# Selective scan of a four-layer network: products made by TensorE, transposing sums, decay factors in SBUF

## The chip, the cores and the metric

The program runs on one core of one Trainium2 chip, in fp32. The metric is the device time of one execution in microseconds (us).

## The reference, cut to what matters

The program computes eight sub-layers in a row (four pairs of a token mixer and a feed-forward part, each with a residual and a layer norm) on a state of 2 x 1024 tokens by 1024 features. The change lies in the mixer of the third pair, a selective scan over time for 2048 channels with 16 states each:

```python
def step(h, inp):
    x_t, dt_t, B_t, C_t = inp
    dA = jnp.exp(dt_t[..., None] * A)
    dBx = dt_t[..., None] * B_t[:, None, :] * x_t[..., None]
    h = dA * h + dBx
    y = jnp.einsum('bdn,bn->bd', h, C_t)
    return (h, y)
h0 = jnp.zeros((x.shape[0], x.shape[1], A.shape[1]), dtype=x.dtype)
_, ys = lax.scan(step, h0, (xT, dtT, BT, CT))
```

The scan's result then gets `D * x` added and is gated by silu(z).

## The kernel before, in words

`l2_scan` (L2552) holds 128 channels on the partitions and 512 tokens on the free axis. The tokens come in CHUNKS = 4 chunks of 512 (chunks 0 and 2 begin a sequence, chunks 1 and 3 start from the saved end state `carry`), the channels in CT = 16 tiles. One tile of one chunk is an **item**; there are 64. The 16 states of an item are taken in pairs (SGR = 2): eight **steps** g = 0 to 7 in an item, 512 steps in all.

One step passes five engines:

- ScalarE makes the decay factors of the pair, two exponentials 128x512 (L2820), into the PSUM ring of five banks.
- GpSimd multiplies dt*x (`dtx`, L2841) by two rows of B, one operation 128x1024 from SBUF into a slot of `h` in SBUF (`make_dBx`, L2851). It runs LEAD = 3 steps ahead; `h` has SLOTS = 6 slots.
- VectorE runs the recurrence, two instructions tensor_tensor_scan (L2921): decay factors from the PSUM ring, products from `h`.
- The product with C follows `KINDS = "YWYWYWYY"`. In a **Y** step VectorE scans into the PSUM ring and multiplies by C into `h` (L2932). In a **W** step it scans into `h`, and GpSimd multiplies `h` by C in place (L2876).
- TensorE adds the pair up in PSUM (`total`, L2753): the identity as weights, 128x512 of `h` moving, two matmuls.

Beside the steps, each item has: TensorE's matmul for dt (L2733) and eight for the gate z (L2743), from chunk 1 on eight matmuls of the output projection of the chunk before (L2538, `OutProj`, whose operands come through a ring of three buffers); ScalarE's softplus and silu (`split`, `log1p`, `gate` with its two table loads L2806 and L2807); VectorE's `pre_c` and `pre_dt` (L2888, L2893), `finish` (L2899, L2902) and, every second item, an addition to the state (L2549); GpSimd's `low` (L2834) and `dtx_`.

Each engine follows an order written by hand, one loop over the steps. GpSimd's loop in step st: `low` (g = 4), `dtx_` (g = 5), `make_dBx(st + 3)`, then in a W step the product with C, which waits for VectorE's scans of that step. In the text below M is such a product with C, and m a product with B. `gate(q - 1)` stands on ScalarE between the exponentials of g = 1 and g = 2 of item q.

In this kernel every instruction of VectorE in the scan that has two tensor inputs takes one of them from PSUM and one from SBUF.

## Time and profile before

| what | value |
|---|---|
| median of 3 runs | 5360.51 us (5357.15 to 5362.31) |
| the profiled execution | 5354.56 us, of which the span is 5352.8 us |
| busy over the whole span | TensorE 92%, VectorE 61%, ScalarE 35%, GpSimd 43% |
| granted TensorE clock, mean | 0.961 |
| the scan | from about 2384 us to 4254 us, more than a third of the span |
| products with B (GpSimd, L2851) | 512, mean 2358 ns |
| products with C (GpSimd, L2876) | 192, mean 2355 ns |
| scans (VectorE, L2921) | 1024, 1205 to 1273 ns |

The shares over the whole span say little: the four engines are busy in different stages. What a change in the scan is worth is read in the scan's own stretch, where the time of one item on each engine can be taken from the starts of its instructions. A start-to-start distance is used for the cost of an instruction where the engine runs without a gap, since the printed durations overlap a little.

### The profile page before, as it was taken

To read this page: it belongs to the slowest core of one execution; us is meant where nothing else is said; L and a number is where in the kernel's file an instruction comes from. 1 tells how busy PE (TensorE), PEld (TensorE's weight loads), DVE (VectorE), ACT (ScalarE), POOL (GpSimd) and SP (SyncE) were. 2 spreads that over 40 slices of the span, in tenths; PEclk is the share of its full clock that TensorE was granted. 3 is DMA by queue.
4 is the path that set the end of the run, shared out by engine and by line. 5 is a ranking of instruction groups with operands and counts; after the bars stand their busy time and mean duration, and the time that the engine had idled before them with its cause. 6 is when DMAs were issued, how large, how long until landed. Compare 5 with 4: busy or idle time off the path is not lost. (4 is left out here: it accounts for less than half of the span.)

```text
span 5352.8 us, 40461 instructions
## 1 busy us (share of the span) xinstructions
...
## 2 busy tenths in 40 slices
...
DMA packets 180006, 360.84 MB, mean 67 GB/s; under 512 B 21790, under 2 KB 56734, under 8 KB 175710
## 3 DMA queue, kind: packets, MB, share of 16 engines
...
## 5 line engine op out<-in xcount | busy, mean ns | idle before, releaser
L2851 POOL TENSOR_TENSOR l2scan_h<-l2scan_dtx,l2scan_Bb 128x1024 f32<-128x1024 f32 x512 | 1198.2, 2358 | 30.8 <-DMA l2scan_Bb<-l_bc 15.0
L2753 PE MATMUL l2scan_yp<-l2scan_h,ident 128*128 128x512 f32 x2048 | 971.5, 608 | 115.1 <-POOL l2scan_h L2876 101.1
L2820 ACT ACTIVATE l2scan_ring<-l2scan_dt,l2scan_A 128x512 f32<-128x512 f32 x1024 | 663.9, 681 | 639.4 <-DVE l2scan_h L2932 481.0
L2753 PEld LDWEIGHTS l2scan_yp<-l2scan_h,ident 128*128 128x128 f32 x2048 | 389.3, 193 | 639.4 <-issue 481.1
L2743 PE MATMUL l2scan_low_z<-state,l2scan_Wz 128*128 128x512 f32 x1024 | 476.6, 598 | 0.3
L2876 POOL TENSOR_TENSOR l2scan_h<-l2scan_h,l2scan_Cb 128x1024 f32<-128x1024 f32 x192 | 452.1, 2355 | 8.6 <-DVE l2scan_h L2921 0.9
L2411 PE MATMUL l2in_acc<-state,l2in_W 128*128 128x512 f32 x1024 | 444.9, 595 | 10.5 <-DMA l2in_W<-l_attn_in_x 10.5
L2932 DVE TENSOR_TENSOR l2scan_h<-l2scan_ring,l2scan_Cb 128x1024 f32<-128x1024 f32 (+1 forms) x384 | 394.3, 1041 | 6.1 <-DMA l2scan_Cb<-l_bc 0.7
L2921 DVE TENSOR_TENSOR_SCAN l2scan_ring<-l2scan_ring,l2scan_carry,l2scan_h 128x512 f32<-128x512 f32 x320 | 392.7, 1273 | 0.0
L2921 DVE TENSOR_TENSOR_SCAN l2scan_ring<-l2scan_ring,l2scan_h 128x512 f32<-128x512 f32 x320 | 373.3, 1212 | 5.5 <-POOL l2scan_h L2851 5.5
L2538 PE MATMUL l2scan_oacc<-l2scan_oy,l2scan_oW 128*128 128x512 f32 x768 | 353.1, 592 | 0.0
L2743 PEld LDWEIGHTS l2scan_low_z<-state,l2scan_Wz 128*128 128x128 f32 x1024 | 197.1, 193 | 256.6 <-issue 255.8
L2411 PEld LDWEIGHTS l2in_acc<-state,l2in_W 128*128 128x128 f32 x1024 | 194.4, 190 | 258.7 <-issue 247.4
L2467 DVE TENSOR_SCALAR l2in_cv<-l2in_xp,l2in_cw,l2in_cb 128x2048 f32<-128x2048 f32 (+1 forms) x17 | 21.8, 1284 | 397.5 <-ACT l2in_xc L2431 354.3
L2921 DVE TENSOR_TENSOR_SCAN l2scan_h<-l2scan_ring,l2scan_carry,l2scan_h 128x512 f32<-128x512 f32 x192 | 235.2, 1267 | 0.0
L2538 PEld LDWEIGHTS l2scan_oacc<-l2scan_oy,l2scan_oW 128*128 128x128 f32 x768 | 145.9, 190 | 183.7 <-issue 183.4
L2198 PE MATMUL l3pair_bank<-state,l3ffn_W 128*128 128x512 f32 x512 | 225.6, 593 | 0.0
L2921 DVE TENSOR_TENSOR_SCAN l2scan_h<-l2scan_ring,l2scan_h 128x512 f32<-128x512 f32 x192 | 223.5, 1205 | 0.6 <-POOL l2scan_h L2851 0.6
L3061 PE MATMUL l2pair_bank<-state,l2ffn_W 128*128 128x512 f32 x512 | 221.6, 592 | 0.0
L2443 ACT ACTIVATE l2in_xp<-l2in_acc 128x512 f32<-128x512 f32 x64 | 38.2, 598 | 482.6 <-PE l2in_acc L2411 482.6
L713 DVE TENSOR_REDUCE l0att_part<-l0att_SB 128x1 f32<-128x512 f32 x192 | 130.9, 690 | 71.9 <-PE l0att_SB L879 71.4
L148 POOL TENSOR_TENSOR l1proj_part<-state 128x1024 f32<-128x1024 f32 x3 | 7.0, 2349 | 383.1 <-DVE state L1704 383.1
...
## 6 DMA issues: line engine op xcount, KB each, us to landing
l2scan_oy<-l_y SPq DMA_DIRECT2D x192, 512.0 KB, 4.9
...
l2scan_oW<-l_attn_out_w SPq DMA_DIRECT2D x192, 128.0 KB, 3.3
...
l2scan_Bb<-l_bc SPq DMA_DIRECT2D x128, 128.0 KB, 6.9
l2scan_Cb<-l_bc SPq DMA_DIRECT2D x128, 128.0 KB, 7.8
...
```

The lines of the kernel that those rows point to most:

```text
L713: v.tensor_reduce(part[:, H % 2, i // 2, i % 2:i % 2 + 1], SB[:, i % 2, :], AX.X, ALU.max, negate=True).then_inc(max_ok, 1)
L2198: t.matmul(acc, self.W[:, k, m * P:(m + 1) * P], x[:, k, :], start=k == 0, stop=False)
L2411: last = t.matmul(acc[:, n % 4, :], W[:, ct % 2, k, :], x[:, k, :], start=k == 0, stop=k == KT - 1)
L2538: last = t.matmul(self.acc, self.W[:, j, k], self.y[:, j, k], start=kp == 0 and k == 0, stop=kp == PIECES - 1 and k == PIECE - 1)
L2743: last = t.matmul(low_z[:, :], Wz[:, q % 2, k, :], x[:, k, :], start=k == 0, stop=k == KT - 1)
L2753: last = t.matmul(yp[:, :], K.ident[:, :], h[:, st % SLOTS, j, :], start=g == 0 and j == 0, stop=g == NSG - 1 and j == SGR - 1)
L2820: a.activation(bank(st, j), dt[:, q % 2, :], ACT.Exp, scale=A[:, ct, n:n + 1]).then_inc(dA_ok, 1)
L2851: g_.tensor_tensor(h[:, st % SLOTS], dtx[:, None, :].to_broadcast([P, SGR, NT]), Bb[:, g * SGR:(g + 1) * SGR, :], ALU.mult).then_inc(dBx_o ...
L2876: g_.tensor_tensor(hs, hs, Cb[:, g * SGR:(g + 1) * SGR, :], ALU.mult).then_inc(hC_g, 1)
L2921: last = v.tensor_tensor_scan(out, bank(st, j), hs[:, j, :], init, ALU.mult, ALU.add)
L2932: last = v.tensor_tensor(hs[:, js], src, Cb[:, g * SGR + js.start:g * SGR + js.stop, :], ALU.mult)
L3061: last = t.matmul(acc, self.W[:, k, m * P:(m + 1) * P], x[:, k, :], start=k == 0, stop=k == KT - 1)
```

## The change

Three things change in `l2_scan`, and buffers move to make room.

1. **Who makes dt*x*B.** Of the eight pairs, two (g = 2 and g = 6, `MAKERS = "PPTPPPTP"`) are made by TensorE. `turn_dtx` transposes dt*x once an item (4 transposes 128x128), ScalarE copies it to SBUF (`keep_dtx`), and `spread` multiplies it with diagonal matrices of B (8 matmuls 128x128 with 128 columns), so that the product comes out with the channels on the partitions, in the PSUM ring. ScalarE makes the diagonals once a chunk (`columns`, `diagonals`: 16 copies 128x128). In these steps the decay factors go to the slot of `h` in SBUF.
2. **The sums.** `total` takes `h` as weights and the identity as moving operand, with is_transpose: 8 passes of 128 columns in place of 2 matmuls of 512 columns. The sum stands transposed in PSUM (`yT`); ScalarE copies it (`keep`), and TensorE turns it back (`turn_back`, 4 transposes). `finish` moves from after g = 1 to after g = 2.
3. **Kinds and buffers.** `KINDS` becomes "YWYWYWYW": one pair more is multiplied by C on GpSimd. The PSUM ring becomes two pairs for the Y steps only. The decay factors of the W steps go to an SBUF buffer of two pairs, `dAw`. `ssm` has one buffer and the ring of the output projection two.

```diff
-KINDS = "YWYWYWYY"
+KINDS = "YWYWYWYW"
+MAKERS = "PPTPPPTP"
...
-        self.RING = 3
+        self.RING = 2
...
-    BANKS = 5
+    PAIRS = 2
...
-        Bb = s.sb("Bb", [P, NS, NT])
+        Bb = s.sb("Bb", [P, SGR * MAKERS.count("P"), NT])
...
+        ysb = l[:, :].rearrange("p (k d) -> p k d", d=P)
+        BT = s.sb("BT", [P, BLOCKS, NS])
+        dtxT = s.sb("dtxT", [P, BLOCKS, P])
+        dg = s.sb("dg", [P, SGR * MAKERS.count("T"), BLOCKS, P])
+        dAw = s.sb("dAw", [P, PAIRS, SGR, NT])
+        ring = s.ps("ring", [P, PAIRS, SGR, NT])
+        yT = s.ps("yT", [P, BLOCKS, P])
...
+        def made(k, st):
+            q, g = divmod(st + 1, NSG)
+            return q * MAKERS.count(k) + MAKERS[:g].count(k)
...
+        def pair(st):
+            return (upto(kind(st), st) - 1) % PAIRS
...
+            return ring[:, pair(st), j, :]
+
+        def wait_pair(e, st):
+            k = kind(st)
+            n = upto(k, st) - PAIRS
+            if n <= 0:
+                return
+            if k == "Y":
+                e.wait_ge(hC_v, n)
+            else:
+                e.wait_ge(h_ok, max(i for i in range(st) if kind(i) == "W" and upto("W", i) == n) + 1)
...
+                        t.wait_ge(copied, q)
+                    for j in range(SGR):
+                        for k in range(BLOCKS):
+                            last = t.matmul(yT[:, k, :], h[:, st % SLOTS, j, k * P:(k + 1) * P], K.ident[:, :], is_transpose=True,
+                                            start=g == 0 and j == 0 and k == 0, stop=g == NSG - 1 and j == SGR - 1 and k == BLOCKS - 1)
+                    last.then_inc(summed, 1)
...
+                def turn_dtx(q):
+                    t.wait_ge(dtx_ok, q + 1)
+                    if q % CT == 0:
+                        t.wait_ge(bt_ok, q // CT + 1)
+                    if q >= 2:
+                        t.wait_ge(y_ok, q - 1)
+                    elif q:
+                        t.wait_ge(dx_ok, q)
+                    for k in range(BLOCKS):
+                        last = t.transpose(yp[:, k * P:(k + 1) * P], dtx[:, k * P:(k + 1) * P], K.ident[:, :])
+                    last.then_inc(dx_ready, 1)
+
+                def spread(st):
+                    q, g = divmod(st, NSG)
+                    n = made("T", st)
+                    t.wait_ge(dg_ok, q // CT + 1)
+                    t.wait_ge(dx_ok, q + 1)
+                    wait_pair(t, st)
+                    for j in range(SGR):
+                        i = SGR * MAKERS[:g].count("T") + j
+                        for k in range(BLOCKS):
+                            last = t.matmul(bank(st, j)[:, k * P:(k + 1) * P], dtxT[:, k, :], dg[:, i, k, :], start=True, stop=True)
+                    last.then_inc(dBxT_ok, 1)
+
+                def turn_back(q):
+                    t.wait_ge(copied, q + 1)
+                    t.wait_ge(dx_ok, min(q + 2, ITEMS))
+                    if q:
                         t.wait_ge(y_ok, q)
-                    for j in range(SGR):
-                        last = t.matmul(yp[:, :], K.ident[:, :], h[:, st % SLOTS, j, :], start=g == 0 and j == 0, stop=g == NSG - 1 and j == SGR - 1)
-                    last.then_inc(summed, 1)
+                    for k in range(BLOCKS):
+                        last = t.transpose(yp[:, k * P:(k + 1) * P], ysb[:, k, :], K.ident[:, :])
+                    last.then_inc(turned_back, 1)
...
+                    if g == 2 and q:
+                        turn_back(q - 1)
...
+                    if st + 1 < STEPS and maker(st + 1) == "T":
+                        spread(st + 1)
...
+                    if g == 6 and q + 1 < ITEMS:
+                        turn_dtx(q + 1)
...
+                def keep(q):
+                    a.wait_ge(summed, (q + 1) * NSG)
+                    a.wait_ge(dt_ok, min(q + 2, ITEMS))
+                    if q:
+                        a.wait_ge(turned_back, q)
+                    a.activation(ysb[:, :, :], yT[:, :, :], ACT.Copy).then_inc(copied, 1)
...
+                def keep_dtx(q):
+                    a.wait_ge(dx_ready, q + 1)
+                    if q:
+                        a.wait_ge(dBxT_ok, made("T", q * NSG - 1))
+                    a.activation(dtxT[:, :, :], yp[:, :].rearrange("p (k d) -> p k d", d=P), ACT.Copy).then_inc(dx_ok, 1)
...
+                def diagonals(c):
+                    a.wait_ge(bt_ok, c + 1)
+                    if c:
+                        a.wait_ge(dBxT_ok, made("T", c * CT * NSG - 1))
+                    for g in range(NSG):
+                        if maker(g) == "P":
+                            continue
+                        for j in range(SGR):
+                            i, n = SGR * MAKERS[:g].count("T") + j, g * SGR + j
+                            for k in range(BLOCKS):
+                                last = a.activation(dg[:, i, k, :], K.ident[:, :], ACT.Copy, scale=BT[:, k, n:n + 1])
+                    last.then_inc(dg_ok, 1)
...
+                    if maker(st) == "P":
+                        wait_pair(a, st)
+                        decay = ring[:, pair(st)] if kind(st) == "Y" else dAw[:, pair(st)]
+                    else:
+                        if st >= SLOTS:
+                            a.wait_ge(summed, st - SLOTS + 1)
+                        decay = h[:, st % SLOTS]
                     for j in range(SGR):
                         n = g * SGR + j
-                        wait_bank(a, st, j)
-                        a.activation(bank(st, j), dt[:, q % 2, :], ACT.Exp, scale=A[:, ct, n:n + 1]).then_inc(dA_ok, 1)
+                        a.activation(decay[:, j, :], dt[:, q % 2, :], ACT.Exp, scale=A[:, ct, n:n + 1]).then_inc(dA_ok, 1)
                     if g == 1 and q:
+                        keep(q - 1)
...
+                    if g == 7 and q + 1 < ITEMS:
+                        keep_dtx(q + 1)
+                        if (q + 1) % CT == 0:
+                            diagonals((q + 1) // CT)
...
+                    if maker(st) == "T":
+                        return
...
-                    v.wait_ge(summed, (q + 1) * NSG)
+                    v.wait_ge(turned_back, q + 1)
...
-                        last = v.tensor_tensor_scan(out, bank(st, j), hs[:, j, :], init, ALU.mult, ALU.add)
+                        if maker(st) == "T":
+                            dA, dBx = hs[:, j, :], bank(st, j)
+                        else:
+                            dA, dBx = bank(st, j) if kind(st) == "Y" else dAw[:, pair(st), j, :], hs[:, j, :]
...
-                        for js, src in runs(st):
-                            last = v.tensor_tensor(hs[:, js], src, Cb[:, g * SGR + js.start:g * SGR + js.stop, :], ALU.mult)
-                        last.then_inc(hC_v, 1)
-                    if g == 1 and q:
+                        v.tensor_tensor(hs, ring[:, pair(st)], Cb[:, g * SGR:(g + 1) * SGR, :], ALU.mult).then_inc(hC_v, 1)
+                    if g == 2 and q:
                         finish(q - 1)
```

The order of GpSimd over one item of chunk 1, from its dt*x (L2841) on. The rows name line, operation, output and inputs. Before:

```order
L2841 TENSOR_TENSOR l2scan_dtx<-l2scan_dt,l2scan_xc 128x512
L2851 TENSOR_TENSOR l2scan_h<-l2scan_dtx,l2scan_Bb 128x1024
L2876 TENSOR_TENSOR l2scan_h<-l2scan_h,l2scan_Cb 128x1024
L2851 TENSOR_TENSOR l2scan_h<-l2scan_dtx,l2scan_Bb 128x1024 x4
L2876 TENSOR_TENSOR l2scan_h<-l2scan_h,l2scan_Cb 128x1024
L2851 TENSOR_TENSOR l2scan_h<-l2scan_dtx,l2scan_Bb 128x1024 x2
L2876 TENSOR_TENSOR l2scan_h<-l2scan_h,l2scan_Cb 128x1024
L2834 TENSOR_TENSOR l2scan_l<-l2scan_l,l2scan_dt 128x512
L2851 TENSOR_TENSOR l2scan_h<-l2scan_dtx,l2scan_Bb 128x1024
```

The same stretch now (L2970 is dt*x, L2982 a product with B, L3007 one with C):

```order
L2970 TENSOR_TENSOR l2scan_dtx<-l2scan_dt,l2scan_xc 128x512
L2982 TENSOR_TENSOR l2scan_h<-l2scan_dtx,l2scan_Bb 128x1024
L3007 TENSOR_TENSOR l2scan_h<-l2scan_h,l2scan_Cb 128x1024
L2982 TENSOR_TENSOR l2scan_h<-l2scan_dtx,l2scan_Bb 128x1024
L3007 TENSOR_TENSOR l2scan_h<-l2scan_h,l2scan_Cb 128x1024
L2982 TENSOR_TENSOR l2scan_h<-l2scan_dtx,l2scan_Bb 128x1024 x2
L3007 TENSOR_TENSOR l2scan_h<-l2scan_h,l2scan_Cb 128x1024
L2982 TENSOR_TENSOR l2scan_h<-l2scan_dtx,l2scan_Bb 128x1024
L3007 TENSOR_TENSOR l2scan_h<-l2scan_h,l2scan_Cb 128x1024
L2962 TENSOR_TENSOR l2scan_l<-l2scan_l,l2scan_dt 128x512
L2982 TENSOR_TENSOR l2scan_h<-l2scan_dtx,l2scan_Bb 128x1024
```

Eight products with B became six and three with C became four, and behind at most two products with B there is now one with C, which waits for VectorE.

VectorE's order from the end of `finish` on (the scans are printed there as SCALAR_TENSOR_TENSOR; L3059 is the scan, L3067 the product with C), now:

```order
L3033 TENSOR_TENSOR l2scan_zs<-l2scan_zs,l2scan_yp 128x512
L3059 SCALAR_TENSOR_TENSOR l2scan_h<-l2scan_dAw,l2scan_carry,l2scan_h 128x512 x2
L3019 SCALAR_TENSOR_TENSOR l2scan_low_z<-l2scan_low_z,l2scan_u 128x512
L3059 SCALAR_TENSOR_TENSOR l2scan_ring<-l2scan_ring,l2scan_carry,l2scan_h 128x512 x2
L3067 TENSOR_TENSOR l2scan_h<-l2scan_ring,l2scan_Cb 128x1024
L3024 TENSOR_TENSOR l2scan_dt<-l2scan_l,l2scan_low_z 128x512
L3059 SCALAR_TENSOR_TENSOR l2scan_h<-l2scan_dAw,l2scan_carry,l2scan_h 128x512 x2
L3059 SCALAR_TENSOR_TENSOR l2scan_ring<-l2scan_h,l2scan_carry,l2scan_ring 128x512 x2
L3067 TENSOR_TENSOR l2scan_h<-l2scan_ring,l2scan_Cb 128x1024
```

Before, the scan of a W step was `l2scan_h<-l2scan_ring,l2scan_carry,l2scan_h`, one input in PSUM; now both inputs, `dAw` and `h`, lie in SBUF. In a step of TensorE's pairs the two inputs changed places, and one of them is still in PSUM.

ScalarE's order from the exponentials of g = 0 to those of g = 3, now:

```order
L2940 ACTIVATE l2scan_ring<-l2scan_dt,l2scan_A 128x512 x2
L2940 ACTIVATE l2scan_dAw<-l2scan_dt,l2scan_A 128x512 x2
L2886 ACTIVATE l2scan_l<-l2scan_yT 128x512
L2892 ACT_TABLE_LOAD
L2892 ACTIVATE l2scan_zs<-l2scan_low_z 128x512
L2893 ACT_TABLE_LOAD
L2940 ACTIVATE l2scan_h<-l2scan_dt,l2scan_A 128x512 x2
L2940 ACTIVATE l2scan_dAw<-l2scan_dt,l2scan_A 128x512 x2
```

The copy of the transposed sum (L2886) is new and stands ahead of the gate and of the exponentials of g = 2; it waits for the last sum of the item before.

## Rows read from the trace of the kernel before

**Rows 1.** Windows: busy us of each engine in a stretch of chunk 0 and chunk 1

```profile
core 0: us, PE busy (x) PEld busy (x) DVE busy (x) ACT busy (x) POOL busy (x), PEclk, DMA share, GB/s
2600.00:2700.00 100.00, 79.39 (x173) 31.83 (x171) 94.60 (x111) 59.80 (x88) 98.38 (x57) 0.98 0.18 45
3000.00:3100.00 100.00, 100.00 (x235) 44.22 (x233) 98.80 (x95) 57.49 (x83) 99.13 (x47) 1.00 0.40 121
```

**Rows 2.** Timeline of VectorE in one item of chunk 1: start, length, instruction

```profile
3012.24 2.46 DVE L2921 TENSOR_TENSOR_SCAN l2scan_ring<-l2scan_ring,l2scan_carry,l2scan_h 128x512 f32<-128x512 f32 x2
...
3015.88 2.45 DVE L2921 TENSOR_TENSOR_SCAN l2scan_h<-l2scan_ring,l2scan_carry,l2scan_h 128x512 f32<-128x512 f32 x2
...
3022.86 0.68 DVE L2893 TENSOR_TENSOR l2scan_dt<-l2scan_l,l2scan_low_z 128x512 f32<-128x512 f32 x1
3023.45 2.45 DVE L2921 TENSOR_TENSOR_SCAN l2scan_h<-l2scan_ring,l2scan_carry,l2scan_h 128x512 f32<-128x512 f32 x2
3025.82 2.44 DVE L2921 TENSOR_TENSOR_SCAN l2scan_ring<-l2scan_ring,l2scan_carry,l2scan_h 128x512 f32<-128x512 f32 x2
...
3029.44 0.68 DVE L2549 TENSOR_TENSOR state<-l2scan_oacc,state 128x512 f32<-128x512 f32 x1
3030.04 2.46 DVE L2921 TENSOR_TENSOR_SCAN l2scan_ring<-l2scan_ring,l2scan_carry,l2scan_h 128x512 f32<-128x512 f32 x2
...
3039.67 0.73 DVE L2899 SCALAR_TENSOR_TENSOR l2scan_yp<-l2scan_xc,l2scan_Dp,l2scan_yp 128x512 f32<-128x512 f32 x1
...
3041.04 2.46 DVE L2921 TENSOR_TENSOR_SCAN l2scan_ring<-l2scan_ring,l2scan_carry,l2scan_h 128x512 f32<-128x512 f32 x2
```

**Rows 3.** Timeline of GpSimd in the same item

```profile
3011.85 2.35 POOL L2876 TENSOR_TENSOR l2scan_h<-l2scan_h,l2scan_Cb 128x1024 f32<-128x1024 f32 x1
3014.16 4.75 POOL L2851 TENSOR_TENSOR l2scan_h<-l2scan_dtx,l2scan_Bb 128x1024 f32<-128x1024 f32 x2
...
3021.18 1.27 POOL L2834 TENSOR_TENSOR l2scan_l<-l2scan_l,l2scan_dt 128x512 f32<-128x512 f32 x1
3022.41 2.36 POOL L2851 TENSOR_TENSOR l2scan_h<-l2scan_dtx,l2scan_Bb 128x1024 f32<-128x1024 f32 x1
3024.93 1.27 POOL L2841 TENSOR_TENSOR l2scan_dtx<-l2scan_dt,l2scan_xc 128x512 f32<-128x512 f32 x1 [0.17 <-POOL l2scan_h L2851]
3026.28 2.35 POOL L2851 TENSOR_TENSOR l2scan_h<-l2scan_dtx,l2scan_Bb 128x1024 f32<-128x1024 f32 x1
```

**Rows 4.** Lines L2899 and L2921: count, min/median/max ns, first and last start

```profile
L2899 DVE SCALAR_TENSOR_TENSOR l2scan_yp<-l2scan_xc,l2scan_Dp,l2scan_yp x64: 727/731/757, 2429.7 to 4252.5; 128x512 f32<-128x512 f32 x64
...
L2921 DVE TENSOR_TENSOR_SCAN l2scan_h<-l2scan_ring,l2scan_carry,l2scan_h x192: 1255/1266/1278, 2862.0 to 4237.6; 128x512 f32<-128x512 f32 x192
```

**Rows 5.** VectorE, line L2019 of another stage: its summary and two of its instructions

```profile
L2019 DVE SCALAR_TENSOR_TENSOR state<-l1ffn_os,l1ffn_b,state x32: 751/753/2626, 1592.9 to 1778.4; 128x512 f32<-128x512 f32 x32
...
1641.01 1.46 DVE L2019 SCALAR_TENSOR_TENSOR state<-l1ffn_os,l1ffn_b,state 128x512 f32<-128x512 f32 x1
...
1684.51 2.60 DVE L2019 SCALAR_TENSOR_TENSOR state<-l1ffn_os,l1ffn_b,state 128x512 f32<-128x512 f32 x1
```

**Rows 6.** Timeline of GpSimd at the same places

```profile
1639.52 2.40 POOL L163 TENSOR_TENSOR l1ffn_sq<-l1ffn_sq 128x1024 f32<-128x1024 f32 x1 [7.31 <-ACT l1ffn_sq L219]
1641.87 2.86 POOL L165 TENSOR_TENSOR l1ffn_sq<-l1ffn_sq 128x1024 f32<-128x1024 f32 x1
...
1684.22 2.34 POOL L154 TENSOR_TENSOR l1ffn_part<-l1ffn_part 128x1024 f32<-128x1024 f32 x1
```

**Rows 7.** Timeline of TensorE in the attention of the last pair

```profile
4822.68 1.04 PE L3176 MATMUL l3att_tp<-ident,l3att_E 128*128 128x128 f32 x8
4823.55 3.74 PE L3186 MATMUL l3att_op<-l3att_PT,l3qkv_vt 128*128 128x128 f32 x32
```

**Rows 8.** Groups of ScalarE by line and shape in the scan, 2600 to 4180 us

```profile
L2820 ACT ACTIVATE l2scan_ring<-l2scan_dt,l2scan_A 128x512 f32<-128x512 f32 x873 | 565.7, 681 | 513.5 <-DVE l2scan_h L2932 392.5 <-DVE l2scan_h L2921 119.2
L2807 ACT ACT_TABLE_LOAD x55 | 70.6, 1283 | 1.0
...
L2806 ACT ACTIVATE l2scan_zs<-l2scan_low_z 128x512 f32<-128x512 f32 x55 | 32.8, 597 | 22.5 <-PE l2scan_low_z L2743 21.4
```

**Rows 9.** Windows of two other stages, for the granted clock

```profile
100.00:150.00 50.00, 40.57 (x131) 23.09 (x130) 20.39 (x28) 10.22 (x19) 2.68 (x10) 0.61 0.00 0
4815.00:4940.00 125.00, 121.31 (x756) 92.35 (x754) 44.18 (x92) 32.91 (x47) 0.10 (x1) 1.00 0.00 1
```

More of the change, by code:

```diff
@@ L2583, in l2_scan @@
         xc_in = [s.sem(f"xc_in{j}") for j in range(3)]
-        ssm_in = [s.sem(f"ssm_in{j}") for j in range(2)]
+        ssm_in = s.sem("ssm_in")
         c_in = [s.sem(f"c_in{g}") for g in range(NSG)]
@@ L2732, in dt_tile @@
                         t.wait_ge(dt_ok, q)
-                    t.matmul(low_z[:, :], Wdt[:, q % 2, :], ssm[:, c % 2, :], start=True, stop=True).then_inc(dt_ready, 1)
+                    t.matmul(low_z[:, :], Wdt[:, q % 2, :], ssm[:, :], start=True, stop=True).then_inc(dt_ready, 1)
                 def z_part(q, k0, k1):
```

82 lines of the change are left out of this document (54 added, 28 removed).

## The prediction

> **What bounds the kernel now.** I looked first at the windows of the scan. In chunk 1 the busy times of 100 us are TensorE 100, GpSimd 99.1 and VectorE 98.8, ScalarE 57 [rows 1]: three engines are full together. In chunk 0, without the output projection, TensorE is busy 79% and GpSimd 98%. Next the length of an item: the first of the 64 `finish` starts at 2429.7 us, the last at 4252.5 [rows 4], so an item takes 1822.8 / 63 = 28.93 us. Then the timelines of one item, read from start to start.
>
> VectorE: a Y step costs 3015.88 - 3012.24 = 3.64 us, a W step 3025.82 - 3023.45 = 2.37, `finish` 1.37, `pre_dt` 0.59 (I take 0.6 for `pre_c` and the addition, of the same size) [rows 2]. Five Y, three W, 1.37, 1.2 and half an addition are 28.2 us.
>
> GpSimd: an operation 128x1024 costs 3014.16 - 3011.85 = 2.31 us, `low` 1.23, dt*x 1.35 and 0.17 ahead of it [rows 3]. Eleven and these are 28.2 us.
>
> TensorE: 235 records in 100 us are 0.4255 us each [rows 1], two to an fp32 matmul, so 0.851 for 512 columns. An item has 1 + 8 + 8 + 16 = 33: 28.1 us, and 21.3 in chunk 0.
>
> **The change, engine by engine.** TensorE: eight transposes start at 4822.68 and what follows them at 4823.55, so one costs 0.109 us, and the 32 records of 16 small matmuls take 3.74 [rows 7]. Eight sums of eight passes are 64 x 0.109 = 7.0 us in place of 16 x 0.851 = 13.6. Two `spread` of 16 records add 3.7, the transposes of dt*x and back 0.9. With 17 large matmuls (14.5) an item is 26.1 us, 19.3 in chunk 0.
>
> GpSimd: six products with B and four with C are 10 x 2.31 = 23.1, with 2.75 for the rest 25.9 us.
>
> VectorE: one Y step becomes a W step: 4 x 3.64 + 4 x 2.37 + 1.37 + 1.2 + 0.3 = 26.9 us, if nothing makes it wait.
>
> By these sums alone an item would fall from 28.9 to about 27 us. ScalarE gets two copies of 0.68 more (its 128x512 exponential to PSUM, mean 681 ns [rows 8]) on 57% of busy time.
>
> **Where a new wait comes from.** The W steps' scans now have both inputs in SBUF, and there are eight an item. The scan stage before has no such instruction, so I looked for one beside a working GpSimd. Line L2019 adds two tensors in SBUF. Its median is 753 ns and its longest 2626 [rows 5]. The long ones lie exactly on GpSimd's operations: one issued at 1684.51, 0.29 us after GpSimd had begun an operation that ended at 1684.22 + 2.34 = 1686.56; it ended at 1687.11, 0.55 us after that [rows 5, 6]. The other way round: one issued at 1641.01 ended at 1642.47, when GpSimd had finished at 1641.92, and GpSimd's next operation, issued at 1641.87, took 2.86 us in place of 2.35 and ended 2.26 us after VectorE's [rows 5, 6]. So the two shut each other out for a whole instruction, and VectorE, waiting, goes ahead of GpSimd's next. An instruction that has waited then takes 0.2 us less than its printed time (0.55 for 0.75), so a scan with carry takes 1.266 - 0.2 = 1.07 us after its wait [rows 4], a GpSimd operation 128x1024 about 2.26.
>
> The Trainium skill (SBUF — State Buffer, Who interferes with whom) states the same as a rule against this change: a VectorE instruction with two SBUF inputs contends with a GpSimd instruction that reads SBUF, and the second to issue is blocked fully. By that rule the item is the one worked out next; without it, that of the first rival. For L2019 the trace agrees (2.60 against 0.75 us); for a scan no run here shows it yet.
>
> **An item with that exclusion**, from the orders of the two engines, each part counted from the end of the W step before. M is a product with C, m one with B; an M starts 0.1 us (my estimate) after the scans it waits for.
> - To the end of W1: VectorE wants it after Y0, at 3.64. GpSimd has M7 to 2.41 and m3 to 4.72. Scan one ends at 5.79, m4 at 8.05, scan two at 9.12.
> - W3: wanted after Y2 and `finish`, at 5.01. GpSimd has M1 and m5, ends at 4.72 and then waits for M3. No collision: 7.38.
> - W5: wanted at 0.6 + 3.64 + 0.59 = 4.83. GpSimd: M3 2.41, `low` 3.64, m7 5.95. Scan one 7.02, dt*x 8.2, scan two 9.27.
> - W7: wanted at 3.94. GpSimd: the blocked m0 2.26, M5 4.57. Scan one 5.64, m1 7.9, scan two 8.97.
>
> The sum is 34.7 us. What stands behind a waiting scan on VectorE (the next Y step, `finish`, `pre_dt`) is late with it, and on GpSimd the products with B stand behind an M that waits for the scans; both delays are in these four parts. The even chunks, whose scans are about 0.06 us shorter but which save `carry` on GpSimd too, come out near 34.9 by the same steps; I take 34.85. GpSimd and VectorE bound each other; neither is full.
>
> The new chain behind M7 stays hidden: M7 2.41, the last sum 1.04, `keep` 0.68, table load 1.28, silu 0.60, table load 1.28, first exponential 0.68 [rows 7, 8] end at 8.0 us; VectorE needs these factors of g = 2 at 9.12. TensorE's 26.1 us lie under 34.85, and the two rings that became shorter (ssm and the projection's) have 9 us of slack an item, so I cost them at nothing; without it a load for the projection would hold up TensorE, the gate and ScalarE. The 16 diagonals of a chunk (0.2 to 0.68 us each, between a fixed cost I estimate and the large copy) hide under the last item's slack in three chunks; the first set is bare with the first transposes: 6 us. Starts of the chunks are loaded as before, with fewer rows of B: nothing.
>
> Sum: (34.85 - 28.93) x 64 = 379, and 6: **385 us**. The profiled execution took 5354.6 us (the span 5352.8, 1.8 around it), which gives 5739.6; the median of the runs lies 5.9 us above it: **5745 us**.
>
> **Bounds.** Under exclusion the shortest item is the time GpSimd and the eight scans need the port one after the other: 10 x 2.26 + 2 x 1.2 + 8 x 1.0 = 33 us, +267, so 5627. The longest is VectorE waiting for a whole operation ahead of each of the eight scans: 26.9 + 8 x 2.3 = 45.3 us, +1050. I stand near the low end because the hand schedule has one of four W steps free and only parts of an operation ahead of the others.
>
> **The rivals.**
>
> *No exclusion for this scan (8%).* For it: the rows show an addition, not a scan. Then the chain above ends last: factors of g = 2 ready at 8.0 us where VectorE wants them at 3.64 + 2.37 = 6.01. VectorE waits 2 us an item: 26.9 + 2.0 = 28.9 with carry, about 28 in the even chunks (scans 0.06 shorter), mean 28.45: -31 us and 6 for the start, 5335. Half a microsecond to one more of wait an item, where TensorE is late with the sums, gives up to 5390.
>
> *The gain as the engine sums have it (3%), the other side.* If there is neither exclusion nor that wait (M7 early, or the gate's 3.2 us before it), VectorE is the bound at 26.9 and 26 us: 2.4 x 64 = 154 us less, near 5205. It decides where the factors of g = 2 are there within 6.0 us of W7's end. The 2.41 + 1.04 + 0.68 + 3.2 of the chain are against it.
>
> *TensorE's clock (6%).* The stretch from 100 to 150 us, with TensorE busy 81%, was granted 0.61, between 1.2 and 2.4 GHz, and the attention of the last pair, busy 97% with transposes among larger matmuls, 1.00 [rows 9]. An item at 34.85 leaves TensorE busy 75%, 55% in chunk 0. At 1.2 GHz throughout it would need 52.2 us (38.6 in chunk 0): 16 x 3.75 + 48 x 17.35 = 893 us over the forecast, near 6640. A fall lengthens its own work and fills the gaps again, so I expect a part of it: 5930 to 6300.
>
> A rule of the Trainium skill speaks for this rival: transposes do not count as TensorE activity for its clock (TensorE: Matmul & The Clock Gate, Part 4). By it the sums' 7 us would be as idle. The 1.00 beside the transposes of the attention shows nothing against it, since these are 8 of every 48 records.
>
> **How the numbers follow.** Exclusion with the schedule above 83%, no exclusion 8%, full gain 3%, clock 6%. The range is that of the likeliest case: from 5640, just above the shortest item, to 5930, where VectorE waits 3 us an item more than I scheduled. It leaves out the rivals and a few in a hundred of the first. A difference of 0.2% (11 us) is about what can be told from no change. Faster: 3% and 2% of the no-exclusion case, 0.05. Within 0.2%: 0.03. Slower: 0.92.
>
> **What the profile after would show.** Right: W scans (output `h`, input `dAw`) of 2 to 3.5 us where they wait, and Y scans unchanged at 1.27; GpSimd's operations partly at 3.3 us in place of 2.36; an item of 34 to 36 us; TensorE near 75% in chunk 1; transposes 0.11 us apart. Wrong: W scans all at 1.2 to 1.3 us (no exclusion), a wait of VectorE's for ScalarE's exponential in g = 2 (the chain behind `keep`), TensorE's clock under 0.8 in the scan with VectorE waiting for `spread`, or waits on the projection's loads.

## The result, and the profile after

| | us | ratio to the kernel before, 95% |
|---|---|---|
| kernel before, median of 4 runs | 5358.89 (5357.15 to 5362.31) | |
| kernel after, median of 4 runs | 5730.69 (5721.73 to 5732.87) | 1.069 (1.0671 to 1.0708) |
| profiled execution after | 5731.06, span 5729.3 | |

The change makes the kernel 372 us slower; 385 were predicted. The profile of after is read in the order of the prediction. First one line of the 64 `finish` (count, min/median/max in ns, first and last start), as in [rows 4]:

```profile
L3030 DVE SCALAR_TENSOR_TENSOR l2scan_yp<-l2scan_xc,l2scan_Dp,l2scan_yp x64: 745/746/755, 2444.5 to 4629.5; 128x512 f32<-128x512 f32 x64
```

An item takes (4629.5 - 2444.5) / 63 = 34.68 us, against 28.93 before. That is 63 x 5.75 = 362 of the 376.5 us by which the span grew (5729.3 - 5352.8). The scan stage begins 7.5 us later in this execution (its operation on A at 2382.4, before at 2374.9). I don't put that down to the change: the same operation stands between 2369.1 and 2383.8 in the kernels below, though the code ahead of it is the same. From it to the first `finish` are 62.1 us, before 54.8, which is the last term, 7.3 us. Only part of it is the start itself: from the operation on A to the first scan are 15.6 us (2382.39 to 2398.01), before 11.2 (2374.93 to 2386.09), 4.5 us more, in which ScalarE's 16 diagonals take 4.77. The rest comes from the first `finish`, which now stands one step later, behind a long W step.

The windows of a stretch in chunk 0 and one in chunk 1 (us; busy time and count of TensorE, its weight loads, VectorE, ScalarE, GpSimd; granted clock, DMA share, GB/s), to hold against [rows 1]:

```profile
2600.00:2700.00 100.00, 69.04 (x351) 53.58 (x349) 99.41 (x82) 51.80 (x78) 84.53 (x47) 0.83 0.14 34
3200.00:3300.00 100.00, 84.20 (x404) 54.09 (x402) 99.48 (x74) 51.93 (x78) 84.14 (x36) 0.94 0.39 113
```

VectorE looks full, at 99%, and nothing else is. But a full engine can be one that stands in its instructions. The line of the scans, form by form, shows it. Each form has one row without `carry` (chunks 0 and 2) and one with it (chunks 1 and 3). The first two rows are the W steps, the other four the Y steps:

```profile
L3059 DVE TENSOR_TENSOR_SCAN l2scan_h<-l2scan_dAw,l2scan_h x256: 1191/2348/3319, 2401.6 to 4073.1; 128x512 f32<-128x512 f32 x128
L3059 DVE TENSOR_TENSOR_SCAN l2scan_h<-l2scan_dAw,l2scan_carry,l2scan_h x256: 1254/2252/3322, 2960.0 to 4623.2; 128x512 f32<-128x512 f32 x128
L3059 DVE TENSOR_TENSOR_SCAN l2scan_ring<-l2scan_ring,l2scan_h x128: 1197/1200/1231, 2398.0 to 4058.6; 128x512 f32<-128x512 f32 x128
L3059 DVE TENSOR_TENSOR_SCAN l2scan_ring<-l2scan_h,l2scan_ring x128: 1195/1197/1229, 2403.8 to 4067.5; 128x512 f32<-128x512 f32 x128
L3059 DVE TENSOR_TENSOR_SCAN l2scan_ring<-l2scan_ring,l2scan_carry,l2scan_h x128: 1258/1264/1292, 2956.3 to 4612.0; 128x512 f32<-128x512 f32 x128
L3059 DVE TENSOR_TENSOR_SCAN l2scan_ring<-l2scan_h,l2scan_carry,l2scan_ring x128: 1253/1257/1291, 2968.8 to 4619.0; 128x512 f32<-128x512 f32 x128
```

The same scan with one input in PSUM never exceeds 1.29 us. With both in SBUF it has a median of 2.25 to 2.35 us and reaches 3.32; its shortest, 1.19, is as short as the others. So it is not a slower instruction but one that waits inside itself, and the views of waits don't show it: the trace lists under 16 us of VectorE waits for this line in the whole stage.

Now VectorE's timeline of one item of chunk 1 (start, us, engine, line, operation, names, count of those run together), the counterpart of [rows 2]:

```profile
3201.04 2.44 DVE L3059 TENSOR_TENSOR_SCAN l2scan_ring<-l2scan_ring,l2scan_carry,l2scan_h 128x512 f32<-128x512 f32 x2
3203.51 1.22 DVE L3067 TENSOR_TENSOR l2scan_h<-l2scan_ring,l2scan_Cb 128x1024 f32<-128x1024 f32 x1
3204.65 5.53 DVE L3059 TENSOR_TENSOR_SCAN l2scan_h<-l2scan_dAw,l2scan_carry,l2scan_h 128x512 f32<-128x512 f32 x2
3210.10 2.43 DVE L3059 TENSOR_TENSOR_SCAN l2scan_ring<-l2scan_h,l2scan_carry,l2scan_ring 128x512 f32<-128x512 f32 x2
...
3215.09 2.45 DVE L3059 TENSOR_TENSOR_SCAN l2scan_h<-l2scan_dAw,l2scan_carry,l2scan_h 128x512 f32<-128x512 f32 x2
3217.46 0.67 DVE L3019 SCALAR_TENSOR_TENSOR l2scan_low_z<-l2scan_low_z,l2scan_u 128x512 f32<-128x512 f32 x1
...
3222.27 4.48 DVE L3059 TENSOR_TENSOR_SCAN l2scan_h<-l2scan_dAw,l2scan_carry,l2scan_h 128x512 f32<-128x512 f32 x2
3226.68 2.43 DVE L3059 TENSOR_TENSOR_SCAN l2scan_ring<-l2scan_h,l2scan_carry,l2scan_ring 128x512 f32<-128x512 f32 x2
...
3230.88 4.65 DVE L3059 TENSOR_TENSOR_SCAN l2scan_h<-l2scan_dAw,l2scan_carry,l2scan_h 128x512 f32<-128x512 f32 x2
3235.45 2.44 DVE L3059 TENSOR_TENSOR_SCAN l2scan_ring<-l2scan_ring,l2scan_carry,l2scan_h 128x512 f32<-128x512 f32 x2
```

and GpSimd's at the same places, the counterpart of [rows 3]; at the end of a row stands how long the engine was idle before it, and what released it:

```profile
3201.19 2.35 POOL L3007 TENSOR_TENSOR l2scan_h<-l2scan_h,l2scan_Cb 128x1024 f32<-128x1024 f32 x1 [1.16 <-DVE l2scan_h L3059]
3203.50 5.60 POOL L2982 TENSOR_TENSOR l2scan_h<-l2scan_dtx,l2scan_Bb 128x1024 f32<-128x1024 f32 x2
3210.26 2.38 POOL L3007 TENSOR_TENSOR l2scan_h<-l2scan_h,l2scan_Cb 128x1024 f32<-128x1024 f32 x1 [1.16 <-DVE l2scan_h L3059]
3212.59 2.38 POOL L2982 TENSOR_TENSOR l2scan_h<-l2scan_dtx,l2scan_Bb 128x1024 f32<-128x1024 f32 x1
3217.62 2.35 POOL L3007 TENSOR_TENSOR l2scan_h<-l2scan_h,l2scan_Cb 128x1024 f32<-128x1024 f32 x1 [2.65 <-DVE l2scan_h L3059]
...
3223.76 1.91 POOL L2970 TENSOR_TENSOR l2scan_dtx<-l2scan_dt,l2scan_xc 128x512 f32<-128x512 f32 x1 [0.23 <-POOL l2scan_h L2982]
3225.75 3.15 POOL L2982 TENSOR_TENSOR l2scan_h<-l2scan_dtx,l2scan_Bb 128x1024 f32<-128x1024 f32 x1
3228.87 2.35 POOL L3007 TENSOR_TENSOR l2scan_h<-l2scan_h,l2scan_Cb 128x1024 f32<-128x1024 f32 x1
3231.18 3.26 POOL L2982 TENSOR_TENSOR l2scan_h<-l2scan_dtx,l2scan_Bb 128x1024 f32<-128x1024 f32 x1
```

Read the two side by side. W1 is issued at 3204.65, 1.15 us into the product m3 that GpSimd began at 3203.50. Its two scans span 5.53 us, and GpSimd's two products m3 and m4 span 5.60 where [rows 3] have 4.75: the instructions stand one after the other. W3 is issued at 3215.09, when GpSimd's last product has ended (3212.59 + 2.38 = 3214.97) and it idles until M3: it takes 2.45, like a Y step's. ScalarE writes decay factors to `dAw` in SBUF during W3 (two exponentials from 3215.28 on), so its writes are not what makes the other W steps long. From the end of one W step to the end of the next (the starts of what follows them: 3201.04, 3210.10, 3217.46, 3226.68, 3235.45):

| part | predicted, us | measured, us |
|---|---|---|
| W1 | 9.12 | 9.06 |
| W3 | 7.38 | 7.36 |
| W5 | 9.27 | 9.22 |
| W7 | 8.97 | 8.77 |
| item | 34.74 | 34.41 |

TensorE is busier than the prediction said, 84% in chunk 1. Three rows of its timeline show why:

```profile
3196.87 1.11 PE L2776 MATMUL l2scan_yT<-ident,l2scan_h 128*128 128x128 f32 x8 [1.90 <-POOL l2scan_h L3007]
3197.80 3.58 PE L2765 MATMUL l2scan_low_z<-state,l2scan_Wz 128*128 128x512 f32 x4
...
3204.52 1.88 PE L2539 MATMUL l2scan_oacc<-l2scan_oy,l2scan_oW 128*128 128x512 f32 x4
```

Four matmul records 128x512 take 3.58 us after an idle of 1.90 and one sum, and 1.88 a little later: nearly twice the time. The granted clock from 3197.80 to 3201.20 is 0.50, the lower of its two levels (1.2 GHz), and from 3204.50 to 3208.00 it is 1.00. The granted clock of the two windows is 0.83 and 0.94, where [rows 1] have 0.98 and 1.00. Nobody pays for it here: VectorE waits for `spread` 2.8 us in all.

### The profile page after: what moved, and what is told of

Its sections match the earlier page's. It is cut to its first block and busy times, and to the rows that moved or that the text cites. A ratio compares the mean times of both kernels' runs of the same rounds, so it can differ in the third digit from the quotient of the medians.

```text
span 5729.3 us, 50163 instructions
## 1 busy us (share of the span) xinstructions
PE 4917.8 (86%) x19120; PEld 2792.8 (49%) x19120; DVE 3686.3 (64%) x3341; ACT 1955.3 (34%) x2873; POOL 2384.1 (42%) x1187
## 5 line engine op out<-in xcount | busy, mean ns | idle before, releaser
L2982 POOL TENSOR_TENSOR l2scan_h<-l2scan_dtx,l2scan_Bb 128x1024 f32<-128x1024 f32 x384 | 1068.8, 2791 | 16.6 <-DMA l2scan_Bb<-l_bc 11.7
L2776 PE MATMUL l2scan_yT<-ident,l2scan_h 128*128 128x128 f32 x4096 | 596.4, 294 | 463.8 <-POOL l2scan_h L3007 463.4
L2776 PEld LDWEIGHTS l2scan_yT<-ident,l2scan_h 128*128 128x128 f32 x4096 | 507.1, 151 | 674.1 <-POOL l2scan_h L3007 545.4
L3007 POOL TENSOR_TENSOR l2scan_h<-l2scan_h,l2scan_Cb 128x1024 f32<-128x1024 f32 x256 | 603.7, 2358 | 177.2 <-DVE l2scan_h L3059 167.0
L3059 DVE TENSOR_TENSOR_SCAN l2scan_h<-l2scan_dAw,l2scan_h 128x512 f32<-128x512 f32 x256 | 585.7, 2327 | 0.0
L3059 DVE TENSOR_TENSOR_SCAN l2scan_h<-l2scan_dAw,l2scan_carry,l2scan_h 128x512 f32<-128x512 f32 x256 | 556.4, 2213 | 0.0
L2940 ACT ACTIVATE l2scan_dAw<-l2scan_dt,l2scan_A 128x512 f32<-128x512 f32 x512 | 338.0, 708 | 5.5 <-DVE l2scan_h L3059 5.5
L3067 DVE TENSOR_TENSOR l2scan_h<-l2scan_ring,l2scan_Cb 128x1024 f32<-128x1024 f32 x256 | 312.3, 1220 | 4.4
L2810 PEld LDWEIGHTS l2scan_ring<-l2scan_dg,l2scan_dtxT 128*128 128x128 f32 x2048 | 296.7, 228 | 32.7 <-issue 27.0
L2810 PE MATMUL l2scan_ring<-l2scan_dg,l2scan_dtxT 128*128 128x128 f32 x2048 | 300.8, 310 | 5.4 <-ACT l2scan_dg L2917 5.4
L2886 ACT ACTIVATE l2scan_l<-l2scan_yT 128x512 f32<-128x512 f32 x64 | 38.2, 597 | 564.6 <-PE l2scan_yT L2776 564.6
```

The source lines that it names most:

```text
L2776: last = t.matmul(yT[:, k, :], h[:, st % SLOTS, j, k * P:(k + 1) * P], K.ident[:, :], is_transpose=True, start=g == 0 and j == 0 and k == ...
L2810: last = t.matmul(bank(st, j)[:, k * P:(k + 1) * P], dtxT[:, k, :], dg[:, i, k, :], start=True, stop=True)
L2940: a.activation(decay[:, j, :], dt[:, q % 2, :], ACT.Exp, scale=A[:, ct, n:n + 1]).then_inc(dA_ok, 1)
L2982: g_.tensor_tensor(h[:, st % SLOTS], dtx[:, None, :].to_broadcast([P, SGR, NT]), Bb[:, rows_at(g), :], ALU.mult).then_inc(dBx_ok, 1)
L3007: g_.tensor_tensor(hs, hs, Cb[:, g * SGR:(g + 1) * SGR, :], ALU.mult).then_inc(hC_g, 1)
L3059: last = v.tensor_tensor_scan(out, dA, dBx, init, ALU.mult, ALU.add)
```

## The experiments

Nine kernels were run. "Exclusion" is the theory of the prediction: a scan with both inputs in SBUF and a GpSimd instruction that reads SBUF shut each other out. The rivals are costs of the other parts of the change. In the runs below the kernel before stood at 5357.6 to 5360.6 us (medians of 7 runs beside each group).

| run | us | ratio, 95% | item, us |
|---|---|---|---|
| decay factors of all steps in PSUM | 5470.51 | 1.0202 (1.0185 to 1.0220) | 30.75 |
| kernel before, W factors in SBUF | 5707.95 | 1.0647 (1.0629 to 1.0664) | 34.46 |
| after, three W steps | 5473.19 | 1.0208 (1.0191 to 1.0225) | 30.70 |
| after, GpSimd only writes | 5425.54 (one run) | | 29.96 |
| all in PSUM, sums as before | 5762.79 | 1.0751 (1.0733 to 1.0769) | 35.40 |
| all in PSUM, gate a step later | 5472.80 | 1.0209 (1.0192 to 1.0226) | 30.73 |
| the same, TensorE's order too | 5426.25 | 1.0124 (1.0107 to 1.0141) | 29.96 |
| that order, W factors in SBUF | 5747.32 | 1.0726 (1.0708 to 1.0744) | 34.98 |
| all in PSUM, three buffers, gate after g = 3 | 5311.86 | 0.9913 (0.9897 to 0.9930) | 28.23 |

### One part alone: the kernel before with the W steps' decay factors in SBUF

```diff
+        dAw = s.sb("dAw", [P, 2, SGR, NT])
...
-                        a.activation(bank(st, j), dt
+                        a.activation(decay(st, j), dt
...
-v.tensor_tensor_scan(out, bank(st, j), hs
+v.tensor_tensor_scan(out, decay(st, j), hs
```

(In this kernel `decay` is the bank in a Y step and a half of `dAw` in a W step. For the room, the ring of the output projection gets two buffers.)

> The kernel before with one part of the change alone: the decay factors of its three W steps go to an SBUF buffer (and the projection's ring has two buffers for room). Exclusion: six scans an item share the port with a full GpSimd: 11 x 2.26 + 2.6 + 6 x 1.05 = 33.8 us at least, about 34.3 an item, 5650 to 5750 us. Rival, the extra time came from TensorE's new work: within 1% of before, W scans at 1.21 to 1.27 us.

5707.95 us: the one part makes 347 of the 372 us. The scans by form:

```profile
L2933 DVE TENSOR_TENSOR_SCAN l2scan_ring<-l2scan_ring,l2scan_h x320: 1197/1206/1232, 2380.3 to 4046.6; 128x512 f32<-128x512 f32 x160
...
L2933 DVE TENSOR_TENSOR_SCAN l2scan_h<-l2scan_dAw,l2scan_h x192: 1192/2222/3414, 2383.9 to 4039.1; 128x512 f32<-128x512 f32 x192
L2933 DVE TENSOR_TENSOR_SCAN l2scan_h<-l2scan_dAw,l2scan_carry,l2scan_h x192: 1250/2240/3431, 2945.7 to 4587.9; 128x512 f32<-128x512 f32 x192
```

No instruction was added here and none moved to another engine; only the place of one operand changed, and the projection's ring is shorter. TensorE is not seen to wait for the projection's loads in this run. This settles the main cause. It does not follow that the rest of the change costs 25 us: parts do not add up when one of them hides the others, as the next run shows.

### The same part undone: all decay factors in PSUM

```diff
-            return (upto(kind(st), st) - 1) % PAIRS
+            return st % PAIRS
...
-                        decay = ring[:, pair(st)] if kind(st) == "Y" else dAw[:, pair(st)]
+                        decay = ring[:, pair(st)]
...
-                            dA, dBx = bank(st, j) if kind(st) == "Y" else dAw[:, pair(st), j, :], hs[:, j, :]
+                            dA, dBx = bank(st, j), hs[:, j, :]
```

> The changed kernel with the decay factors of the W steps back in PSUM (one ring of two pairs for all steps), so that no scan has both inputs in SBUF; all else as changed. Exclusion of VectorE and GpSimd: W scans fall from a mean of 2.2 to 2.3 us to 1.21 to 1.27, an item from 34.7 us to about 28.7 (VectorE's 26.9 and the 2 us that the factors of g = 2 are late behind the copy of the sum and the gate), the kernel to 5300 to 5400 us. Rival, the extra time comes from TensorE's chains or its clock: the kernel stays above 5650 us and VectorE waits for TensorE or ScalarE instead.

5470.51 us: 260 less than after, but 110 more than before, where 5300 to 5400 were expected. The long scans are gone, and a wait stands in their place:

```profile
L3057 DVE TENSOR_TENSOR_SCAN l2scan_h<-l2scan_ring,l2scan_h x256: 1195/1204/1218, 2396.9 to 3872.2; 128x512 f32<-128x512 f32 x128
L3057 DVE TENSOR_TENSOR_SCAN l2scan_h<-l2scan_ring,l2scan_carry,l2scan_h x256: 1253/1266/1278, 2890.3 to 4366.0; 128x512 f32<-128x512 f32 x128
...
  ACT l2scan_h L2938: 246.7, 63
```

The last row is VectorE's wait (us in total, times), 3.9 us an item, for the decay factors of g = 2, which ScalarE makes after the gate. VectorE's own work by the prediction is 26.9 us an item with `carry` and 26 without, in the mean 26.45. With 3.9 and about 0.5 of other waits this is the item of 30.75. The chain behind M7 in one item, on GpSimd, TensorE and ScalarE, and VectorE's row that waits for it:

```profile
3224.32 2.36 POOL L3005 TENSOR_TENSOR l2scan_h<-l2scan_h,l2scan_Cb 128x1024 f32<-128x1024 f32 x1
...
3226.47 1.91 PE L2774 MATMUL l2scan_yT<-ident,l2scan_h 128*128 128x128 f32 x16
...
3228.41 0.60 ACT L2884 ACTIVATE l2scan_l<-l2scan_yT 128x512 f32<-128x512 f32 x1 [3.38 <-PE l2scan_yT L2774]
3229.03 1.28 ACT L2890 ACT_TABLE_LOAD   x1
3230.32 0.60 ACT L2890 ACTIVATE l2scan_zs<-l2scan_low_z 128x512 f32<-128x512 f32 x1
3230.94 1.28 ACT L2891 ACT_TABLE_LOAD   x1
3232.23 1.33 ACT L2938 ACTIVATE l2scan_h<-l2scan_dt,l2scan_A 128x512 f32<-128x512 f32 x2
...
3233.09 2.46 DVE L3057 TENSOR_TENSOR_SCAN l2scan_ring<-l2scan_h,l2scan_carry,l2scan_ring 128x512 f32<-128x512 f32 x2 [3.41 <-ACT l2scan_h L2938]
```

W7 ended at 3223.61. M7 starts 0.7 us behind it, since the product m1 stood ahead of it on GpSimd. It ends at about 3226.65, but the 16 passes on TensorE are two sums: that of g = 6 runs first (0.87 us, to 3227.34), another 0.7 us late. The factors are taken at 3233.09, 9.5 us after W7's end. In after the same chain took 8.2 (from 3235.45, W7's end, to the first exponential of g = 2, 3242.96 + 0.68), and VectorE wanted its result only after 9.06 us, W1's length. So exclusion hid this chain.

### How much per W step: three in place of four

```diff
-KINDS = "YWYWYWYW"
+KINDS = "YWYWYWYY"
```

> The changed kernel with KINDS as before, YWYWYWYY: six scans with two SBUF inputs an item in place of eight. Exclusion: from the end of W5 to the end of the next W1 the schedule gives 13.7 us in place of 18.1, an item about 30.3 us, 5400 to 5500 us in all. Rival, a loss that goes with TensorE's pairs and sums: within 1% of the changed kernel's 5730 us.

5473.19 us, an item of 30.70; the schedule by the prediction's rules gave 30.3. W scans with carry have a median of 1277 ns and a longest of 2626, without carry 1524 and 3314: fewer of them meet a product. The longest without `carry` is as long as before, the longest with it shorter (2626 against 3322). One W step changed to a Y step gains 258 us, though it adds 1.27 us of VectorE's own work an item; it also takes one product with C from GpSimd.

### Reading or writing: GpSimd's products replaced by fills

This kernel leaves out GpSimd's products with B and with C: each is replaced by two fills with zero (memset) of its output, so GpSimd only writes there; `low` and `dtx_` stay.

```diff
-                    g_.tensor_tensor(hs, hs, Cb[:, g * SGR:(g + 1) * SGR, :], ALU.mult).then_inc(hC_g, 1)
+                    glink(g_.memset(hs, 0.0))
+                    g_.memset(hs, 0.0).then_inc(hC_g, 1)
```

> The changed kernel in which GpSimd's products with B and C are left out: each is replaced by two memsets of the same slot of h (so the scan works on zeros and the kernel's output is not the reference's); dt*x and the addition for dt stay. GpSimd then writes SBUF about 10 x 1.9 us an item and hardly reads it. If only GpSimd's reads shut out VectorE: W scans at 1.21 to 1.27 us but for those beside the two small operations that are left, an item of 27 to 29 us, 5230 to 5360 us. If its writes do as well: W scans with a median above 1.5 us, an item above 30 us, over 5420 us.

The W scans fall to a median of 1215 and 1275 ns. GpSimd's and VectorE's rows of one place:

```profile
3203.25 0.95 POOL L2984 MEMSET l2scan_h<- 128x1024 f32 x1
3204.43 1.68 POOL L2971 TENSOR_TENSOR l2scan_dtx<-l2scan_dt,l2scan_xc 128x512 f32<-128x512 f32 x1 [0.23 <-POOL l2scan_h L2984]
...
3209.98 0.95 POOL L2983 MEMSET l2scan_h<- 128x1024 f32 x1
3210.99 0.95 POOL L2984 MEMSET l2scan_h<- 128x1024 f32 x1
```

```profile
3203.78 3.42 DVE L3062 TENSOR_TENSOR_SCAN l2scan_h<-l2scan_dAw,l2scan_carry,l2scan_h 128x512 f32<-128x512 f32 x2
...
3210.72 2.45 DVE L3062 TENSOR_TENSOR_SCAN l2scan_h<-l2scan_dAw,l2scan_carry,l2scan_h 128x512 f32<-128x512 f32 x2
```

Beside the fills two W scans take 2.45 us and the fills stay at 0.95: neither waits. The pair that takes 3.42 meets the product dt*x, which reads SBUF and takes 1.68 there. This holds for the whole stage: of the 248 pairs of W scans that the timeline prints as one row, 62 take more than 2.6 us, and each of them overlaps a dt*x. Of the other 186, none overlaps a product or an addition on GpSimd, and 121 overlap a fill. So GpSimd's operations that read SBUF exclude the scan, and fills, which only write, don't. The time, 5425.54, is above the expected 5230 to 5360 and even above the 5420 set for exclusion by writes, though the scans rule that out. The cause is the chain found in the kernel with all factors in PSUM: VectorE waits 160.4 us, 2.5 an item, for the factors of g = 2.

### What the transposing sums bring: all in PSUM, sums as before

`total` is the two matmuls of 512 columns again; `keep` and `turn_back` are gone, as `finish` reads the sum directly.

```diff
-                            last = t.matmul(yT[:, k, :], h[:, st % SLOTS, j, k * P:(k + 1) * P], K.ident[:, :], is_transpose=True,
...
+                        last = t.matmul(yT[:, :], K.ident[:, :], h[:, st % SLOTS, j, :], start=g == 0 and j == 0, stop=g == NSG - 1 and j == SGR - 1)
```

> The shared ring with the sums as before (identity as weights, two matmuls of 512 columns), without the copy and the turn back: TensorE needs 26.1 - 7.0 - 0.4 + 13.6 = 32.3 us an item in chunks 1 to 3, 25.4 in chunk 0, and nothing waits for the copy of the sum. It becomes the bound: 48 x (32.3 - 28.9) - 16 x 1.5 + 6 = 145 us over before, 5450 to 5550 us. If it is no slower than the shared ring with transposing sums, these bring nothing here.

5762.79 us, where 5450 to 5550 were expected. VectorE waits 529.1 us for `spread` (8.3 an item): TensorE, 92% busy in the window of chunk 1, holds it up. By the prediction's prices its work there is 33 matmuls, 28.1 us, and 4.1 for the products and their transposes, 32.2 in all. It also waits, which I had not added:

```profile
PE l2scan_yT L2772 <- DVE l2scan_zs L3005: 195.7, 63, 4.4
```

This is TensorE's first sum of an item waiting for `finish` of the item before, which reads the same bank: 3.1 us an item. In the kernel before, where `finish` stands after g = 1, the same wait is 12.1 us in the whole stage; this run leaves `finish` after g = 2. So the 292 us between this kernel and the one with all factors in PSUM are not the price of the sums alone. They hold the longer matmuls (6.2 us of TensorE's work an item by the prediction's prices) and this wait, and the two were not measured apart.

### Moving the gate: three orders

Three kernels, all with the factors in PSUM, tried to hide the chain behind M7. First `keep`, `gate`, `turn_back`, `finish` and the matmul for dt one step later, and the last sum no longer pulled ahead.

```diff
-                    if g == 1 and q:
+                    if g == 2 and q:
                         keep(q - 1)
```

> As the shared ring, and the copy of the sum, the gate, the turn back, the matmul for dt and the finish all stand one step later, and the last sum is not pulled ahead. If the chain last sum, copy, gate, factors of g = 2 is what holds the shared ring above VectorE's own 26.9 us, an item falls to 27 to 28 us, 5220 to 5330 us, below the kernel before. If TensorE (26.1 us of work in an item) or its clock is the bound there, it is no faster than the shared ring.

5472.80 us: no gain, where 5220 to 5330 were expected. The wait for the factors of g = 2 went. In its place VectorE waits 183.3 us for TensorE's products and 68.6 for the input of `pre_c` from ScalarE. TensorE at one place:

```profile
3214.93 1.91 PE L2774 MATMUL l2scan_yT<-ident,l2scan_h 128*128 128x128 f32 x16
3220.34 3.60 PE L2808 MATMUL l2scan_ring<-l2scan_dg,l2scan_dtxT 128*128 128x128 f32 x16 [3.50 <-DVE l2scan_h L3063]
```

TensorE waited 3.5 us for the ring (two pairs, so the product of a Y step must be done first), then ran the 16 records in 3.60 us, where 1.95 is usual; the granted clock from 3220.30 to 3223.90 is 0.54. So TensorE is idle for the short ring, runs at the lower clock behind it, and VectorE waits for the result.

Then TensorE's order as well: `spread` for g = 2 ahead of the sum, the projection's matmuls two steps later, `pre_c` a step later.

```diff
+                    if g == 1:
+                        spread(st + 1)
                     if st >= 2:
                         total(st - 2)
-                    if q >= CT and proj.before(q) + g < proj.before(q + 1):
-                        proj.matmuls(t, proj.before(q) + g)
+                    if q >= CT and g >= 2 and proj.before(q) + g - 2 < proj.before(q + 1):
+                        proj.matmuls(t, proj.before(q) + g - 2)
```

> The shared ring with the later gate, and three moves more: the products of g = 2 stand on TensorE ahead of the last sum, the projection's matmuls stand two steps later (in the gap before the products of g = 6), and VectorE's first operation for dt stands after the Y step of g = 4. If the 30.7 us an item of both shared rings are waits of VectorE for factors and products (3 to 4 us an item in their traces), an item falls to 27 to 28.3 us and the kernel to 5240 to 5330 us, below before. If the two pairs of the ring are too few for any order (TensorE's 26.1 us of work behind VectorE's Y products, its clock falling in the gap), an item stays above 29.5 us, 5400 us or more.

5426.25 us, 47 better, but still above before and above the expected 5240 to 5330. VectorE now waits 1.8 us an item for the factors of g = 3, and the projection for its load:

```profile
3212.24 3.63 PE L2539 MATMUL l2scan_oacc<-l2scan_oy,l2scan_oW 128*128 128x512 f32 x4 [2.33 <-DMA l2scan_oy<-l_y]
```

TensorE waits 68.0 us in all for these loads. That is the ring of two buffers that the prediction costed at nothing. The same order on the changed kernel, with the W factors left in SBUF:

> The changed kernel, decay factors of the W steps in SBUF as it has them, with the same reordering as the run before. Exclusion alone sets its item (the chain behind the copy of the sum was hidden): within 1% of the changed kernel's 5731 us, W scans at 2.2 to 2.3 us in the mean. If the order of TensorE and ScalarE had a part in the 34.7 us, it falls by more than 60 us.

5747.32 us, within 1% of the changed kernel as expected: under exclusion the order is worth nothing. W scans have a mean of 2286 and 2194 ns between 2700 and 4500 us. At last three buffers for the projection again, and `keep` and `gate` after the exponentials of g = 3, all factors in PSUM:

```diff
-        self.RING = 2
+        self.RING = 3
...
-                    if g == 2 and q:
+                    if g == 3 and q:
                         keep(q - 1)
```

> The reordered shared ring with two waits more taken out: the projection's ring has three buffers again (the SBUF room of the decay factors is free), and the copy of the sum and the gate stand behind the exponentials of g = 3. Its trace still shows 1.8 us an item of VectorE waiting for the factors of g = 3 and 2.8 us for the products of g = 6, behind a projection matmul that waited for its operands and then ran at half the clock. Without these an item falls from 30.0 us to 27.2 to 28.5 us and the kernel to 5250 to 5340 us, below before. If TensorE's own 26.1 us in a fixed order is the bound, an item stays above 29 us, 5360 us or more.

5311.86 us, ratio 0.9913 (0.9897 to 0.9930), in the expected range: nearly 1% faster than the kernel before. Its `finish` line and its windows:

```profile
L3028 DVE SCALAR_TENSOR_TENSOR l2scan_yp<-l2scan_xc,l2scan_Dp,l2scan_yp x64: 729/754/757, 2438.0 to 4216.4; 128x512 f32<-128x512 f32 x64
```

```profile
2600.00:2700.00 100.00, 83.18 (x448) 62.49 (x447) 95.62 (x105) 64.71 (x98) 97.57 (x61) 0.91 0.17 40
3200.00:3300.00 100.00, 92.09 (x476) 61.39 (x475) 92.75 (x85) 62.46 (x105) 87.44 (x41) 0.99 0.57 158
```

An item takes (4216.4 - 2438.0) / 63 = 28.23 us, 0.70 under before: 44 us over 63 items, the 46 us between the medians. The two edits of this run were not tried apart. VectorE still waits 42.8 us in all for `spread` and 21.2 for the projection; with 26.45 us of its own work an item in the mean, up to 1.8 are left.

## Why the prediction was right, point by point

- **The engine sums.** VectorE's work, 26.9 us with `carry` and 26 without, is borne out by the run with all factors in PSUM: 30.75 less 3.9 for the factors of g = 2 and 0.5 of other waits is 26.4 in the mean. `spread` took 1.79 us from start to start (3206.24 to 3208.03 in after's timeline of TensorE) for the 1.87 estimated, a sum of eight passes 0.87, as 8 x 0.109.
- **The exclusion** was read off one line of another stage, an addition [rows 5, 6], and held for the scan. The Trainium skill (SBUF — State Buffer, Who interferes with whom) says that a VectorE instruction with two SBUF inputs contends with a GpSimd instruction that reads SBUF, and not with one that only writes it. Both halves agree with the runs here: 2.25 to 2.35 us in place of 1.2 to 1.27 beside products, 2.45 for two beside fills. The one part alone costs 347 us.
- **The schedule of the item.** 34.85 us predicted, 34.68 measured over all items, and each of the four parts of the item read within 0.2 us. It was worth working out part by part: the bounds alone allowed 33 to 45 us.
- **The start**, 6 us predicted for the first transposes and diagonals, was 4.5 up to the first scan. The 7.3 to the first `finish` also holds the later place of `finish`, so it does not confirm this term. The sum came out 13 us too high (385 for 372): the item was 0.17 us too long over 64 items, 11 us, and the start 1.5.
- **The chain behind M7** in the changed kernel: 8.0 us predicted, 8.2 in the item read, hidden under W1's 9.06, as predicted.
- **The chain in the first rival** was mis-sized. "The factors of g = 2 ready at 8.0 us" holds only where GpSimd and TensorE are free when M7 and the last sum come. Without exclusion M7 stood 0.7 us behind m1 and the last sum 0.7 behind that of g = 6, and it was 9.5 us. The rival's 5335 to 5390 would have been missed: 5470 was measured with a shared ring of two pairs, and 5426 with fills, whose M is even shorter. I had priced the chain by its own links, without what is queued ahead of each on its engine.
- **TensorE "75%" in chunk 1** was mis-sized: 84%. The 26.1 us are right at the full clock; at 0.94 and 0.83, with four records in 3.58 us in place of 1.88, it was more. The clock rival, put at 6%, came in part and cost nothing, because TensorE had slack.
- **The two shorter rings at nothing** was right for the changed kernel (the projection waits 4.8 us in all for its loads) and wrong without exclusion: TensorE waits 68.0 us for these loads in the reordered kernel, 2.33 in the item read. The prediction had made the 9 us of slack an item its condition. The shorter ring of `ssm` was not tried alone.

What stays open: how much of the last run's gain each of its two edits makes, what the transposing sums are worth by themselves, and whether a ring of three pairs in PSUM would bring VectorE's own 26.45 us; there was no room in PSUM, and it was not tried. The runs don't settle either whether transposing passes count for the granted clock as other matmuls do, which the prediction's clock rival rests on: the low stretches read here all stand behind idle times.
